# Down products 6 to 11 of the feed-forward part in seven block products instead of six tile products, with their sums added to the result in DRAM by accumulating transfers

## The reference, cut to what matters

```
xn  = layernorm(x)
att = softmax_causal((h @ Wq) @ (h @ Wk).T / sqrt(512)) @ (h @ Wv) @ Wo + xn     # h = layernorm(xn) * gamma + beta
g   = silu(xn @ w_gate) * (xn @ w_up)                                            # 2048 x 2048
g   = g where |g| is among the two largest of its group of 4 columns, else 0
out = x + att + g @ w_down                                                       # w_down: 2048 x 512
```

## Time and profile before

| | us |
|---|---|
| runs shown, median of 3 | 789.2 |
| the profiled execution, its own time | 788.73 |
| its span, first to last instruction | 786.9 |
| PE busy | 783.3 |
| DVE, ACT, POOL busy | 610.2, 319.0, 16.7 |

### The profile page before, as it was taken

How to read it: one execution, slowest core, us unless ns; L and a number is a source line. 1 busy time by engine, 2 the same in 40 slices (tenths; PEclk the granted TensorE clock), 3 DMA queues, 4 the chain that set the end, 5 groups by cost and what they waited for, 6 DMA issues and landing times.

```text
span 786.9 us, 9292 instructions
## 1 busy us (share of the span) xinstructions
PE 783.3 (100%) x3518; PEld 648.6 (82%) x3518; DVE 610.2 (78%) x964; ACT 319.0 (41%) x514; POOL 16.7 (2%) x26
## 2 busy tenths in 40 slices
PE   9999999999999999999999999999999999999998
PEld 6888888888888888888888888888888888888887
DVE  6988789678635797689989789898657658659786
ACT  5432250234123473464643634463423424335431
POOL 2011110010000000000000000000000000000000
PEclk9999999999999999999999999999999999999999
DMA  9441704500131543684464352797276163161002
GB/s 325 183 162 55 242 0 184 189 2 1 54 101 35 213 184 111 205 340 176 189 210 181 142 202 93 282 338 291 78 284 260 44 241 136 51 241 55 0 1 107
DMA packets 31611, 121.74 MB, mean 155 GB/s; under 512 B 3088, under 2 KB 3664, under 8 KB 29136
## 3 DMA queue, kind: packets, MB, share of 16 engines
q1 hardware_dynamic: 30272, 119.00, 40.9%
q10 hardware_dynamic: 1296, 2.16, 0.8%
HBM read 77.07 MB, written 44.07 MB: 154 GB/s over the span
## 4 chain that ended last, share of the span: by engine, by line
PE 100%; DVE 0%; issue 0%
PE bank L962 13%; PE bank L963 13%; PE bank L961 13%; PE bank L701 10%; PE bank L699 10%; PE bank L700 10%; PE bank L838 8%; PE bank L1041 7%; PE bank L1042 7%; PE bank L1043 7%; PE bank L903 0%; PE bank L709 0%; PE bank L804 0%; PE bank L771 0%; PE bank L1054 0%; PE bank L1053 0%
## 5 line engine op out<-in xcount | busy, mean ns | idle before, releaser
L961 PE MATMUL bank<-X_hi,wset 128*128 128x512 f32 x448 | 174.4, 389 | 0.0
L963 PE MATMUL bank<-X_hi,wset 128*128 128x512 f32 x448 | 174.3, 389 | 0.0
L962 PE MATMUL bank<-X_lo,wset 128*128 128x512 f32 x448 | 174.3, 389 | 0.0
L961 PEld LDWEIGHTS bank<-X_hi,wset 128*128 128x128 f32 x448 | 84.1, 188 | 17.7 <-issue 0.2
L962 PEld LDWEIGHTS bank<-X_lo,wset 128*128 128x128 f32 x448 | 84.1, 188 | 17.5
L963 PEld LDWEIGHTS bank<-X_hi,wset 128*128 128x128 f32 x448 | 84.1, 188 | 17.3
L1041 PE MATMUL bank<-dw,hs_hi 128*128 128x512 f32 x224 | 87.2, 389 | 0.0
L1042 PE MATMUL bank<-dw,hs_hi 128*128 128x512 f32 x224 | 87.1, 389 | 0.0
L1043 PE MATMUL bank<-dw,hs_lo 128*128 128x512 f32 x224 | 87.1, 389 | 0.0
L1675 DVE TENSOR_TENSOR acc<-bank,acc 128x512 f32<-128x512 f32 x59 | 40.1, 687 | 40.0 <-PE bank L1043 39.6
L699 PE MATMUL bank<-zg,xT 128*128 128x512 f32 (+2 forms) x132 | 49.8, 377 | 0.0
(11 more groups left out here) (259 smaller groups left out, 1444.3 us busy)
## 6 DMA issues: line engine op xcount, KB each, us to landing
w_operands<-wset SPq DMA_DIRECT2D x8, 3584.0 KB, 13.4
wset<-w_operands SPq DMA_DIRECT2D x8, 3584.0 KB, 12.1
wsum<-w_units SPq DMA_DIRECT2D x28, 256.0 KB, 3.8
dw_raw<-L_ffn_w_down SPq DMA_DIRECT2D x14, 512.0 KB, 5.0
xw<-L_attn_x SPq DMA_DIRECT2D x4, 1024.0 KB, 9.6
xt_raw<-x_t SPq DMA_DIRECT2D x8, 512.0 KB, 8.9
xn_t<-xt_raw SPq DMA_DIRECT2D x8, 512.0 KB, 2.8
acc<-resid SPq DMA_DIRECT2D x2, 2048.0 KB, 9.6
```

Of the source, the lines that this page charges most:

```text
L961: pe.matmul(dst[:], u[:, 0, :], x_hi, start=(first and kt == 0), stop=False, skip_group_check=True)
L962: pe.matmul(dst[:], u[:, 0, :], x_lo, start=False, stop=False, skip_group_check=True)
L963: last = pe.matmul(dst[:], u[:, 1, :], x_hi, start=False, stop=(kt == 1), skip_group_check=True)
```

## The change

Down products 6 to 11 (`BLOCKED`) become seven block products each: the kept hidden values (512 rows by 512) and the slice of w_down (512 by 512) are cut into 2 by 2 blocks, and P1 to P7 are made from sums of blocks (`D_A11` ... for the left, `D_B11` ... for the right). Each block product is 2 x 2 x 3 = 12 matmuls of 256 columns, 84 for a down product.

- The right operands (three slices, two pieces each, pieces 0 to 5) are made once: POOL loads w_down, DVE makes 4 sums (`prep_sums`), ACT 2 casts (`prep_operands_hi`), DVE 2 low parts (`prep_operands_lo`), POOL stores to DRAM. Pieces 0 to 3 lie in the attention part, piece 4 (`PREP_FIRST`) in stage 0, piece 5 (`PREP_LATE`) in stage 3 and its end. SP loads them to `dwop` when they are needed.
- The left operands are made in the stage: DVE 4 sums and 7 low parts, ACT 7 casts.
- The partial sums leave PSUM by 7 ACT copies (`keep_part`); DVE adds the two halves that belong together (`sum_staged`).
- `acc` is used for the last two down products alone. The rows go straight to the result (`out_tiles`), and for down products 0 to 12 the sum is staged in SBUF, two tiles at a time, and POOL adds it to the result with an accumulating DMA (26 of 512 KB). For those of the 13 that aren't blocked, ACT copies the four tiles (`keep_down`) in place of DVE's add, or DVE does (`take_down`, down products 0 and 5).

```diff
+BLOCKED = range(6, 12)
+FIRST_OPS = 4
+D_A11, D_S3, D_S2, D_A12, D_S1, D_A22, D_S4 = range(7)
+D_P1, D_P7, D_P6, D_P2, D_P5, D_P4, D_P3 = range(1, 8)
+D_B11, D_T3, D_T2, D_B21, D_T1, D_T4, D_B22 = range(7)
...
-      *u[4:6], xn[2][1], xn_store[2], u[6], xh_pre[3][0], u[7], xh_pre[3][1], xh[3][0], u[8], xh_pre[3][2], xh[3][1], u[9],
...
+      *prep_sum[0], *u[4:6], *prep_hi_steps[0], xn[2][1], xn_store[2], u[6], xh_pre[3][0], u[7], xh_pre[3][1], xh[3][0], u[8], xh_pre[3][2], xh[3][1], u[9],
...
+    def load_blocked(q, halves=(0, 1)):
+        i = BLOCKED[0] + 2 * q - 1
+        for h in halves:
+            some = (slice(0, FIRST_OPS), slice(FIRST_OPS, NOP))[h]
+            if q:
+                sp.wait_ge(part_full, NOP * block_no(i) + some.stop)
+            elif h == 0:
+                sp.wait_ge(prep_stored, 16 * 2 * N_PREP)
+            else:
+                sp.wait_ge(*product_done(i))
+            sp.dma_start(dwop[:].bitcast(F32)[:, some].rearrange("p o r h d -> p o r (h d)"), dwop_dram[q][:, some]).then_inc(dwop_loaded[h], 16)
...
             sp.wait_ge(rows_ready, n + 1)
-            sp.dma_start(resid_dram[n], row_slot(n)).then_inc(resid_stored[n % 2], 16)
+            sp.dma_start(out_tiles[n], row_slot(n)).then_inc(resid_stored[n % 2], 16)
...
+    def load_prep(p):
+        prep, prep_raw = prep_at(p)
+        j, r = (BLOCKED[0] // 2 + p // 2) % NJ, p % 2
+        if p == 0:
+            pool.wait_ge(blocks_stored, 64)
+            pool.wait_ge(xn_ready[0], 2)
+        else:
+            pool.wait_ge(prep_stored, 16 * p)
+        nc.gpsimd.dma_start(prep_raw[:, D_B11:D_T3 + 1, 1, :], down_units[j, 0][:, r, :].rearrange("p (o d) -> p o d", o=2)).then_inc(prep_loaded, 16)
+        nc.gpsimd.dma_start(prep_raw[:, D_B21:D_B22 + 1:D_B22 - D_B21, 1, :], down_units[j, 1][:, r, :].rearrange("p (o d) -> p o d", o=2)
+                     ).then_inc(prep_loaded, 16)
+    def store_prep(p):
+        prep, prep_raw = prep_at(p)
+        pool.wait_ge(prep_ready, 2 * (p + 1))
+        nc.gpsimd.dma_start(dwop_dram[p // 2][:, :, p % 2, :], prep[:].bitcast(F32).rearrange("p o h d -> p o (h d)")).then_inc(prep_stored, 16)
...
+    store_prep(PREP_FIRST)
+    load_prep(PREP_LATE)
+    for stored in resid_stored:
+        pool.wait_ge(stored, 8 * NT)
+    for i in range(N_DMA):
+        for b in range(2):
+            tile = (i // NQ) * 2 * TC + (i % 2) * TC + 2 * b
+            if i not in BLOCKED:
+                pool.wait_ge(*bank_copied(i, 2 * b + 1))
+            elif b == 0:
+                pool.wait_ge(part_kept, NOP * (block_no(i) + 1))
+            else:
+                pool.wait_ge(staged_summed, block_no(i) + 1)
+            if (i, b) == (2, 0):
+                store_prep(PREP_LATE)
+            nc.gpsimd.dma_start(out_tiles[tile:tile + 2].rearrange("t p d -> p t d"), staged[b][:], accum_op=ALU.add
+                                ).then_inc(pair_added[b], 16)
...
+    def blocked_part(i, k, op, first):
+        dst = down_bank_blocked(k)
+        pe.wait_ge(op_ready, NOP * block_no(i) + op + 1)
+        if i % 2 == 0:
+            pe.wait_ge(dwop_loaded[0 if op < FIRST_OPS else 1], 16 * (block_no(i) // 2 + 1))
+        for t in range(2):
+            for r in range(2):
+                s_hi, s_lo = (half[op][:, r, t * P:(t + 1) * P] for half in (op_hi, op_lo))
+                d_h, d_l = dwop[:, op, r, 0, :], dwop[:, op, r, 1, :]
+                out_half = dst[:, t * (W // 2):(t + 1) * (W // 2)]
+                pe.matmul(out_half, s_hi, d_h, start=(first and t == r == 0), stop=False, skip_group_check=True)
+                pe.matmul(out_half, s_hi, d_l, start=False, stop=False, skip_group_check=True)
+                last = pe.matmul(out_half, s_lo, d_h, start=False, stop=(r == 1), skip_group_check=True)
+        last.then_inc(part_full, 1)
...
+    def down_blocked(i):
+        kept_before = NOP * block_no(i)
+        if kept_before:
+            pe.wait_ge(part_kept, kept_before)
+        else:
+            pe.wait_ge(*bank_copied(i - 1, TC - 1))
+        blocked_part(i, D_P1, D_A11, True)
+        pe.wait_ge(silu_ready, 4 * (i + 2) + 1)
+        pe.wait_ge(hid_ready, 4 * (i + 2) + 1)
+        blocked_part(i, D_P7, D_S3, True)
+        pe.wait_ge(part_kept, kept_before + 1)
+        blocked_part(i, D_P6, D_S2, False)
+        blocked_part(i, D_P2, D_A12, False)
+        pe.wait_ge(part_kept, kept_before + 3)
+        blocked_part(i, D_P5, D_S1, False)
+        pe.wait_ge(part_kept, kept_before + 2)
+        blocked_part(i, D_P4, D_A22, False)
+        pe.wait_ge(part_kept, kept_before + 5)
+        blocked_part(i, D_P3, D_S4, False)
...
+    def prep_operands_hi(p, k):
+        prep, prep_raw = prep_at(p)
+        act.wait_ge(prep_step, 4 * (p + 1))
+        some = (slice(0, 3), slice(3, NOP))[k]
+        nc.scalar.copy(prep[:, some, 0, :], prep_raw[:, some, 1, :]).then_inc(prep_hi, 1)
...
+    def keep_down(i, t):
+        if t % 2 == 0:
+            act.wait_ge(pair_added[t // 2], 16 * i)
+        act.wait_ge(down_full, TC * whole_no(i) + t + 1)
+        nc.scalar.copy(staged[t // 2][:, t % 2, :], down_bank(i, t)[:]).then_inc(down_kept, 1)
...
+    def keep_part(i, k):
+        act.wait_ge(part_full, NOP * block_no(i) + k)
+        src = down_bank_blocked(k)[:]
+        if k == D_P1:
+            nc.scalar.copy(bank[7][:], src).then_inc(part_kept, 1)
+            return
+        b, half = {D_P7: (2, 1), D_P6: (1, 0), D_P2: (0, 0), D_P5: (1, 1), D_P4: (2, 0), D_P3: (0, 1)}[k]
+        if k == D_P2:
+            act.wait_ge(pair_added[0], 16 * i)
+        elif k == D_P7:
+            act.wait_ge(staged_summed, block_no(i))
+        elif k == D_P6:
+            act.wait_ge(pair_added[1], 16 * i)
+        nc.scalar.copy(staged[b][:, :, half * (W // 2):(half + 1) * (W // 2)], src.rearrange("p (t d) -> p t d", t=2)).then_inc(part_kept, 1)
...
         if n:
             act.wait_ge(hid_ready, 4 * (n - 1) + 3)
         nc.scalar.activation(g_sum[3][:], bank[0][:], ACT.Silu).then_inc(silu_ready, 1)
+        if n == 0:
+            prep_operands_hi(PREP_FIRST, 0)
+            prep_operands_hi(PREP_FIRST, 1)
...
+        if i in BLOCKED:
+            operand_hi(i, D_S1)
+            keep_part(i, D_P1)
+            operand_hi(i, D_A22)
         last_silu(n)
-        if n == 2:
+        if i in BLOCKED:
+            keep_part(i, D_P7)
+            keep_part(i, D_P6)
+            operand_hi(i, D_S4)
+            keep_part(i, D_P2)
+            keep_part(i, D_P5)
+            keep_part(i, D_P4)
+            magnitudes(i + 1, (0, 1))
+            keep_part(i, D_P3)
+        elif n == 2:
             for m in range(4):
...
+        elif 2 < n < N_Q - 1:
+            for t in range(TC):
+                keep_down(i, t)
+            if n == 3:
+                prep_operands_hi(PREP_LATE, 0)
+                prep_operands_hi(PREP_LATE, 1)
...
+    def prep_sums(p, k):
+        prep, prep_raw = prep_at(p)
+        b11, b12, b21, b22, t2, t1, t4 = (prep_raw[:, o, 1, :] for o in (D_B11, D_T3, D_B21, D_B22, D_T2, D_T1, D_T4))
+        if k == 0:
+            dve.wait_ge(prep_loaded, 32 * (p + 1))
+            nc.vector.tensor_tensor(t1, b12, b11, ALU.subtract).then_inc(prep_step, 1)
+            nc.vector.tensor_tensor(b12, b22, b12, ALU.subtract).then_inc(prep_step, 1)
+        else:
+            dve.wait_ge(prep_step, 4 * p + 1)
+            nc.vector.tensor_tensor(t2, b22, t1, ALU.subtract).then_inc(prep_step, 1)
+            dve.wait_ge(prep_step, 4 * p + 3)
+            nc.vector.tensor_tensor(t4, b21, t2, ALU.subtract).then_inc(prep_step, 1)
+    def prep_operands_lo(p, k):
+        some = (slice(0, 3), slice(3, NOP))[k]
+        prep, prep_raw = prep_at(p)
+        dve.wait_ge(prep_hi, 2 * p + k + 1)
+        nc.vector.tensor_tensor(prep[:, some, 1, :], prep_raw[:, some, 1, :], prep[:, some, 0, :].bitcast(F32),
+                                ALU.subtract).then_inc(prep_ready, 1)
...
+    def operand_sums(i):
+        a11, a12, a21, a22 = blocks_a(i)
+        done = 4 * block_no(i)
+        dve.wait_ge(picked, G * (i + 1))
+        nc.vector.tensor_tensor(op_raw[D_S3][:], a11, a21, ALU.subtract).then_inc(op_step, 1)
+        nc.vector.tensor_tensor(op_raw[D_S1][:], a21, a22, ALU.add).then_inc(op_step, 1)
+        dve.wait_ge(op_step, done + 2)
+        nc.vector.tensor_tensor(op_raw[D_S2][:], op_raw[D_S1][:], a11, ALU.subtract).then_inc(op_step, 1)
+        dve.wait_ge(op_step, done + 3)
+        nc.vector.tensor_tensor(a21, a12, op_raw[D_S2][:], ALU.subtract).then_inc(op_step, 1)
...
+    def sum_staged(i):
+        dve.wait_ge(part_kept, NOP * block_no(i) + D_P4)
+        nc.vector.tensor_tensor(staged[1][:], staged[1][:], staged[2][:], ALU.add).then_inc(staged_summed, 1)
...
         nc.vector.tensor_tensor(b_tile(n, 0)[:], g_sum[3][:], bank[1][:], ALU.mult).then_inc(hid_ready, 1)
+        if n == 0:
+            prep_sums(PREP_FIRST, 0)
+            prep_sums(PREP_FIRST, 1)
+        if i in BLOCKED:
```

(15 more changed lines are left out.)

271 lines of the change are left out of this document (186 added, 85 removed).

## The result

The changed kernel takes 799.98 us (median of 4 runs, 798.63 to 800.95), the kernel before 789.36 in the same comparison: ratio 1.0134, interval 1.0116 to 1.0151. It is slower, and the forecast of 787.7 (785.0 to 790.6) was wrong.

A forecast was written before the change was run, and what follows sets the result against it. PE was taken as the bound, busy 783.3 of 786.9 us. 788.73 - 5.2 + 2.0 + 1.6 = 787.1 for the profiled execution; 0.47 for the median and a tenth for thin covers gave 787.7, range 785.0 to 790.6.

The forecast's parts named there:

- The work that goes: PE in the six blocked down products: 10.0 us instead of 10.88 each, 0.87 less, 5.2 us saved in all.
- Pieces 0 to 3: Attention part: added DVE, ACT and transfer work hidden, counted as nothing; 1 to 2 us if it slips.
- The width rule: Matmul gap of N/2.4 + 2.5 ns, from the Trainium skill: the six products would save 7.1 us.
- The third wide softmax: Tightest place in the attention part: low part 2.3 us later, still 0.5 us early, no wait counted.
- The signs that the prediction named for being wrong: Two gaps missing, ACT waiting before a copy of P6 or P2, or a 256-column matmul over 0.123 us.
- nowhere else above 0.3: Expected sign: PE idle about 2 us near 326.7 and 1.4 near 405, no other idle above 0.3 us.
- Piece 4: Stage 0 to 1: DVE's sums and ACT's casts delay gate_seed of stage 1; PE waits 2.0 us.
- Piece 5: Stage 3 to 4: casts delay gate_seed, PE waits 1.4 us, then 0.2 for up_seed; 1.6 together.
- Accumulating transfers: Two pairs per blocked product: 2 x 6 = 12 us, hidden within 22 us; landing expected within 12 us.
- The first two: Rivals: casts of both or one pair cause no wait, 784.1 to 786.1, chance 0.15; accumulating transfers don't fit, 796, chance 0.08.
- Pieces come late: Rival, attention part: POOL's transfers and DVE hinder each other, 1 to 4 us, 789 to 792; chance 0.12.
- The clock rival: PE's clock falls after the first wait; four microseconds at the lower level lose about 2: 789.7; chance 0.05.

The follow-up runs named there:

- e2: Changed kernel without pieces 0 to 3; down products 6 to 9 read the operands of 10 and 11, so part of the result differs: 789.20 us, ratio 1.0003.
- e9: e6 with the narrow warm-up matmuls of e7, the whole computation: 785.13 us, ratio 0.9951 to the kernel before.
- e10: e9 without the hold on piece 2's store, which goes out as soon as its low parts are made: 786.82 us, ratio 0.9973.
- e11: e9 with piece 2's sums back ahead of the row tiles and only its store held: 785.89 us, ratio 0.9959.
- e8: Changed kernel with only down products 10 and 11 blocked, two pieces placed as in e5, none in the attention part: 788.69 us, ratio 0.9996.
- e7: Changed kernel with 28 warm-up matmuls of 128 columns instead of 7 of 512 at the start of PE's program: 796.37 us, ratio 1.0092.
- e3: Changed kernel with pieces 0 to 3 made but not stored; down products 6 to 9 read other operands, result partly wrong: 791.20 us, ratio 1.0028.
- e6: Changed kernel with e5's moves, piece 2's sums behind the row tiles, its store and piece 4's load held back; whole computation: 787.66 us, ratio 0.9984.
- e1: Changed kernel with the casts and low parts of pieces 4 and 5 later in stages 1 and 4: 797.46 us, ratio 1.0102.
- e4: Changed kernel with the load of piece 0 held until rows 6 and 7 have landed: 803.69 us, ratio 1.0180.
- e5: As e2, with sums, casts and low parts of pieces 4 and 5 also moved on ACT and DVE: 785.33 us, ratio 0.9952.

## Why the prediction was wrong

**The work that goes: right, slightly over.** 0.81 us a product against 0.87 forecast (0.1199 us a matmul, not 0.119), the first 0.60; 4.5 in all with 0.1 of small waits, not 5.2. The width rule gave 7.1; the measured pitch decided.

**Pieces 0 to 3: the step that failed.** "I count nothing; if it slips, 1 to 2 us" measured 10.9 us in the trace (3.8 near 164, 5.9 near 248, 1.3 near 316), and e2 shows that it was theirs: 10.8 us between the medians. The third wide softmax, which I called the tightest place, held. I had asked whether each piece came in time for its own use ("Piece stores (1792 KB, about 7 us) and loads have 20 us and more"), and not what its transfers do to others:
- Near 248 the store of piece 2 and SP's weight loads share the DMA engines. e9 against e10 shows this, since the hold is the only edit between them, and e11 shows that the hold alone is enough. The Trainium skill (DMA: Bandwidth & Descriptors, Issuing engines are not separate DMA queues) says that transfers started by SP, ACT or POOL run on the same 16 engines and interleave; the traces agree, with 8.1 us against 3.7.
- Near 164 two things meet, the instruction packet and piece 0's work. The packet without pieces cost nothing (e2) or 0.1 us (e8), the pieces without the packet under the stores 0.4 us (e7) or nothing (e3, e9); together they cost 3.8 us (2.1 in e6, 1.9 in e1). A shift of 1.2 us in four stores grew to 2.2 in the landing of the row store behind them; SP waits for that landing before the next row load, and DVE for that row. It grew to 1.9 in e8 as well, without pieces, so up to that point it is not the pieces' doing. What piece 0's work does, as far as the traces tell, is to take the time in which DVE would catch up: the second of the two xn_t stores that follow goes out at 155.3 us in e8, as in the kernel before (155.2), and at 157.9 in the changed kernel. Which part of that work was not tried, beyond the load in e4. The Trainium skill (the same page, Why a DMA increments its semaphore by 16 and not by 1) says that a transfer's parts finish independently and the semaphore counts them; the landing of all four stores 1.2 us late, with one engine held 1.7 us, agrees.
- Near 316 the load of T4 landed late: issued at 307.8 us, it took 6.5 us instead of 3.3. The stop is gone in e2, e3 and e6. In e6 T4's load and the store of piece 3 have the same places in the program as in the changed kernel, but the load of piece 4 is held until T4 has landed, and T4 took 5.0 us; in the changed kernel that load went out at 303.6, beside it. So it was the load of piece 4, as far as the traces tell; no run has that hold alone.

The signs that the prediction named for being wrong all stayed away: the two gaps came, ACT waited for PE alone before the copies of partial sums, and a matmul of 256 columns took 0.1199 us. What showed it was its "nowhere else above 0.3": PE stood idle at three other places.

**Piece 4: the wait right, its follow-up missed.** The stop measured 1.98 us against 2.0 forecast, but then the slow matmuls cost 1.6. I had this as a rival with 0.05, "short beside the 3 us of warm-up"; it happened in the profiled execution of the changed kernel, and five of e2's ten runs had a lowered clock. e1 and e5 show the parts: ACT's order 1.1 us and the clock, DVE's order the rest.

**Piece 5: right.** 1.33 and 0.2 forecast as 1.4 and 0.2; e1 and e5 show the cause.

**Accumulating transfers: right.** 5.5 us a pair in the median for 6 forecast; nothing waited for them. But four of the 26 took over the 12 us that the prediction allowed (12.1, 12.5, 17.8, 20.6), so the cover held and the single time did not. What the staging adds elsewhere is at most the 0.6 us of e8 between 520 and 560, whose cause stays open.

**The rivals.** The first two did not come: both pairs of casts held PE up, and no accumulating transfer did. "Pieces come late" named the right part, priced at 1 to 4 us, and with the wrong mechanism: DVE's copies and POOL's descriptors. Its highest price was 4 us, and 10.8 came, slow matmuls included. The clock rival had the right mechanism, priced at 2 us for one fall; three falls cost about 1.6 us each. The covers in the blocked stages held.

Open: why the row store behind block_sums landed in 6.3 us in e4 and e8 and in 4.7 in e2, the packet at 131 in all three; where the packet fell in the executions that were not profiled; and which part of PE's program a packet holds, since 42 instructions moved it by 13 us.

## What to carry to other kernels

Work put into idle stretches has to be charged for its transfers too: list which loads land in the same microseconds and who waits for them, and hold a store that nobody needs until those have landed. Where a chain goes through a landing, then a queue, then an engine in order, slack is not additive: two delays that cost at most 0.1 and 0.4 us alone cost 1.9 to 3.8 us together. A stop of PE of 2 us may cost twice its length, so remove it even where the work that causes it pays.
